# Gated cross-attention and FP4 feed-forward on one core: bias products summed by VectorE, the weights' power applied at the copies, another order of the first tiles

## What is computed

```python
# attention
kp = ctx @ Wk.T;  vp = ctx @ Wv.T + bv;  qp = layernorm(x) @ Wq.T + bq
probs = softmax(qp @ kp.T / sqrt(512))
x = x + tanh(g_xattn) * ((probs @ vp) @ Wo.T + bo)
# feed-forward, 512 -> 1408 -> 512; q4 rounds blocks of 16 to FP4 values
h = silu(q4(layernorm(x)) @ q4(w_gate).T) * (q4(layernorm(x)) @ q4(w_up).T)
x = x + tanh(g_ffn) * (q4(h) @ q4(w_down).T)
```

## Time and profile before

| | |
|---|---|
| median of 3 runs | 832.83 us (832.35 to 833.42) |
| span of the profiled execution | 832.3 us |
| TensorE busy | 822.4 us, 99% |
| VectorE busy | 650.7 us, 78% |
| ScalarE busy | 459.9 us, 55% |
| GpSimd busy | 400.5 us, 48% |
| granted TensorE clock, mean | 1.000 of full speed |
| chain that ended last: TensorE's share | 93% |
| of it `product` (L1918) / `down` (L2037) | 60% / 27% |

### The profile page before, as it was taken

The page is one execution under the profiler, slowest core; times in us unless marked ns, Lnnn a source line. Parts: engine busy times, 40 slices in busy tenths (PEclk is TensorE's granted clock), DMA queues, the critical chain, the costliest instruction groups (busy, mean ns, idle before and its releaser), DMA issues.

```text
span 832.3 us, 11653 instructions
## 1 busy us (share of the span) xinstructions
PE 822.4 (99%) x4102; PEld 417.0 (50%) x4102; DVE 650.7 (78%) x967; ACT 459.9 (55%) x930; POOL 400.5 (48%) x333
## 2 busy tenths in 40 slices
PE   9999999999999999999999999999999999999998
PEld 5555445444554445444544454445544454444445
DVE  5887899898998698877878688778876878776654
ACT  2778675547555666456563755366646565344320
POOL 3498797764334353444333543454444533444421
PEclk9999999999999999999999999999999999999999
DMA  9723703553243434532641255224433443222232
GB/s 318 285 70 103 157 13 97 122 128 92 48 80 106 108 82 89 129 56 54 114 120 40 55 110 136 61 60 99 97 61 61 85 85 73 58 54 55 48 75 73
DMA packets 192817, 78.21 MB, mean 94 GB/s; under 512 B 176387, under 2 KB 178037, under 8 KB 192759
## 3 DMA queue, kind: packets, MB, share of 16 engines
q1 hardware_dynamic: 192759, 77.47, 39.6%
HBM read 22.76 MB, written 8.39 MB: 37 GB/s over the span
## 4 chain that ended last, share of the span: by engine, by line
PE 93%; ACT 3%; DVE 2%; issue 1%; DMA 1%; POOL 1%; POOLq 0%; ACTq 0%; DVEq 0%
PE banks L1918 60%; PE banks L2037 27%; DVE banks L1417 1%; PE banks L2053 1%; PE banks L1912 1%; PE banks L1971 1%; PE banks L1999 1%; PE banks L1998 1%; PE banks L2143 1%; DMA x_T<-x_parts 1%; PE banks L2150 0%; PE banks L2008 0%; PE banks L2160 0%; PE banks L2165 0%; PE banks L2155 0%
## 5 line engine op out<-in xcount | busy, mean ns | idle before, releaser
L1918 PE MATMUL banks<-wgu_hi,x_T 128*128 128x512 f16 (+1 forms) x1536 | 439.3, 361 | 1.6 <-DMA x_T<-x_parts 0.9
L1918 PE MATMUL banks<-wgu_lo,x_T 128*128 128x512 f16 (+1 forms) x768 | 277.5, 361 | 0.0
L1918 PEld LDWEIGHTS banks<-wgu_hi,x_T 128*128 128x128 f16 x1536 | 150.3, 98 | 155.6 <-issue 1.3
L2037 PE MATMUL banks<-wd,arena 128*128 128x512 f16 x1023 | 227.2, 379 | 0.0
L2037 PEld LDWEIGHTS banks<-wd,arena 128*128 128x128 f16 x1023 | 99.7, 98 | 117.4 <-issue 0.6
L648 POOL TENSOR_TENSOR arena<-arena,h_r 128x1024 f32<-128x1024 f32 (+1 forms) x60 | 93.2, 1554 | 115.3 <-DVE h_r L1372 115.3
L648 POOL TENSOR_TENSOR arena<-arena,h_s 128x1024 f32<-128x1024 f32 x64 | 90.7, 1418 | 88.6 <-DVE arena L1419 53.6
L1918 PEld LDWEIGHTS banks<-wgu_lo,x_T 128*128 128x128 f16 x768 | 75.1, 98 | 76.8 <-issue 0.3
L648 POOL TENSOR_TENSOR xwork<-xwork,x_s 128x512 f32<-128x512 f32 x32 | 38.4, 1201 | 152.0 <-DVE xwork L1419 152.0
L1052 ACT ACTIVATE arena<-banks,scal 128x512 f32<-128x512 f32 (+1 forms) x96 | 61.9, 647 | 84.9 <-PE banks L1918 84.8
L1571 DVE SCALAR_TENSOR_TENSOR arena<-arena,scal,banks 128x512 f32<-128x512 f32 (+1 forms) x90 | 62.2, 694 | 56.3 <-PE banks L1918 53.5
(11 more groups left out here) (199 smaller groups left out, 1043.6 us busy)
## 6 DMA issues: line engine op xcount, KB each, us to landing
ring<-in_x_dram SPq DMA_DIRECT2D x8, 1024.0 KB, 5.1
out_dram<-ring SPq DMA_DIRECT2D x31, 256.0 KB, 2.2
arena<-in_L_ffn_w_down_dram SPq DMA_DIRECT2D x4, 704.0 KB, 5.0
arena<-in_L_ffn_w_gate_dram SPq DMA_DIRECT2D x5, 512.0 KB, 9.7
arena<-in_L_ffn_w_up_dram SPq DMA_DIRECT2D x5, 512.0 KB, 9.6
ring<-in_L_xattn_Wk_dram SPq DMA_DIRECT2D x4, 256.0 KB, 6.1
ring<-in_L_xattn_Wq_dram SPq DMA_DIRECT2D x4, 256.0 KB, 6.8
wd<-in_ctx_dram SPq DMA_DIRECT2D x1, 1024.0 KB
```

What stands on the lines that cost most here:

```text
L1918: ended = e.matmul(at, l, r, start=(i == 0), stop=(i == len(terms) - 1))
L2037: ended = e.matmul(by_k(down_ps(t)[:, :], KD), l, r, start=(k == 0 and i == 0), stop=(k == KH - 1 and i == 2))
```

## The change

What it does, part by part:

- **Bias terms.** VectorE sums the four slices of k, each times its bias entries as a per-partition factor (`weighted`: one tensor_scalar, three scalar_tensor_tensor): `bq_sum` over Wk, `key_sum` over the context for both halves at once (616 columns), `bv_sum` over Wo. The sum over partitions is one product with a matrix of ones. The row product of bq, its copy, and the turns go; four products with a one-column moving operand make `bqk_col`. The sums lie in `xn1` and `prob_bytes`, which is why `ln1_apply(0)` and `prob_copy` get a wait. The two bias products of the keys follow each other (`KEY_ORDER`). Wv's load waits for `bq_sum`.
- **Global power.** For pairs 0 to 5 `gu_folds` no longer takes the power, only the constant DOWN, so `gu_times` needs no `pow_ready`. `gu_high` and `gu_low` become activations with the factor `inv_gu`, and the subtracted identity holds minus the power (`neg_p`, one more operation in `gu_power`; `scale_ident` on ScalarE).
- **Squares.** `sum_ps` is renamed `square_ps`; the squares go where they went.
- **Order.** All five lists are ordered anew up to tile 6: among others VectorE has `key_sum`, `scale_bo`, `gu_scales(5)` and `gu_scales(6)` ahead of `gu_top_of`, `gu_round(2)` ahead of `power_of('gu')`, `gu_round(3)` and `gu_round(4)` ahead of `gu_power`; TensorE has `key_product(3)` behind `top_turn('gu')`; ScalarE has `ln1_apply(0)` and `key_copy(5)` behind the first `gu_high`, and `ln1_stats(1)` right ahead of `exps(0)`; SyncE has `x_turn(1)` behind three `move_values`, and the first stores earlier. The loop from tile 7 on is unchanged.

```diff
         ident = sb("ident", [P, P])
-        neg_ident = sb("neg_ident", [P, P], F16)
-        ones = sb("ones", [1, P])
+        neg_ident = sb("neg_ident", [P, P], BF16)
+        ones = sb("ones", [P, P])
...
+        neg_p = sb("neg_p", [P, 1])
...
-        bqk_row = probT[0:1, :]
+        bq_sums = xn1[:, 0, :]
+        key_sums = xn1[:, 1:3, :].rearrange("p i n -> p (i n)")[:, 0:ROWS]
+        bv_sums = prob_bytes[:, :]
...
-        sum_ps = banks[:, 6 * BANK:8 * BANK]
         att_ps = bank[5]
+        square_ps = banks[:, 6 * BANK:8 * BANK]
...
+        KEY_ORDER = [(0, m) for m in range(KD)] + [(0, KD), (1, KD)] + [(1, m) for m in range(KD)]
+        mm = [("key", i) for i in range(KEYS_HALF)] + [("vo", m) for m in range(KD)] + [("bvwo", 0)]
...
             e.dma_start(stage_b, by_rows(Wo)).then_inc(loads["wo"], 16)
-            w.wait_ge(bqk_mm, 1)
+            w.wait_ge(bq_summed, 1)
             e.dma_start(stage_a, by_rows(Wv)).then_inc(loads["wv"], 16)
...
             x_turn(0)
-            x_turn(1)
             move_values(1)
             move_values(2)
-            x_turn(2)
             move_values(3)
-            move_down(0)
+            x_turn(1)
             move_values(4)
             move_values(5)
             move_values(6)
+            move_down(0)
             move_values(7)
+            x_turn(2)
             move_down(1)
             move_down(2)
             move_down(3)
             x_turn(3)
-            h_turn(0)
             w.wait_ge(h_div[1], 2)
             load_x(3)
+            h_turn(0)
             h_turn(1)
             x_turn(4)
...
+            gu_times(0)
             gu_divide(4)
+            gu_times(1)
             gu_divide(5)
             gu_divide(6)
+            gu_times(2)
             ln1(0)
-            gu_times(0)
-            gu_times(1)
-            gu_times(2)
+            gu_divide(7)
             gu_times(3)
-            gu_divide(7)
             gu_divide(8)
             gu_times(4)
-            gu_divide(9)
             gu_times(5)
             gu_times(6)
+            gu_divide(9)
+            gu_divide(10)
             gu_times(7)
             gu_times(8)
-            gu_divide(10)
             gu_low_of(6)
             gu_low_of(7)
+            gu_low_of(8)
             gu_times(9)
-            gu_low_of(8)
             gu_low_of(9)
             x_stats(0)
             gu_times(10)
+            x_stats(1)
+            gu_low_of(10)
...
+                if j0 < MOVED:
+                    e.activation(gu_s[:, cols], gu_s[:, cols], ACT.Copy, scale=DOWN).then_inc(gu_fold, j1 - j0)
+                    return
                 w.wait_ge(pow_ready, NTH["gu"])
                 e.activation(gu_s[:, cols], gu_s[:, cols], ACT.Copy, scale=fold_gu[:, :]).then_inc(gu_fold, j1 - j0)
 
+            def scale_ident():
+                w.wait_ge(consts, IDENT)
+                w.wait_ge(pow_ready, NTH["gu"])
+                e.activation(neg_ident[:, :], ident[:, :], ACT.Copy, scale=neg_p[:, :]).then_inc(negated, 1)
+
             def gu_high(n):
                 w.wait_ge(gu_turned, n + 1)
-                e.copy(wgu_hi[:, gu_at(n), :, :], by_k(bank[gu_bank(n)][:, 0:D], KD)).then_inc(gu_hi, 1)
+                w.wait_ge(pow_ready, NTH["gu"])
+                e.activation(wgu_hi[:, gu_at(n), :, :], by_k(bank[gu_bank(n)][:, 0:D], KD), ACT.Copy, scale=inv_gu).then_inc(gu_hi, 1)
 
             def gu_low(n):
                 w.wait_ge(gu_less, n + 1)
-                e.copy(wgu_lo[:, gu_at(n), :, :], by_k(bank[gu_bank(n)][:, 0:D], KD)).then_inc(gu_lo, 1)
+                e.activation(wgu_lo[:, gu_at(n), :, :], by_k(bank[gu_bank(n)][:, 0:D], KD), ACT.Copy, scale=inv_gu).then_inc(gu_lo, 1)
...
+                if b == 0:
+                    w.wait_ge(bqk_mm, 1)
+                    w.wait_ge(key_mm, KEYS_HALF + 1)
...
             def key_copy(i):
-                j, m = divmod(i, KEYS_HALF)
+                j, m = KEY_ORDER[i]
                 w.wait_ge(key_mm, i + 1)
                 to = keyq[:, m, j * HALF:(j + 1) * HALF] if m < KD else keyb[:, j * HALF:(j + 1) * HALF]
                 e.mul(to, bank[mm_bank["key", i]][:, 0:HALF], SOFT).then_inc(key_sb, 1)
...
-            w.wait_ge(consts, IDENT)
-            e.activation(neg_ident[:, :], ident[:, :], ACT.Copy, scale=-1.0).then_inc(negated, 1)
             gu_squares(0)
             gu_squares(1)
+            gu_folds(0, 2)
...
             w.wait_ge(bqk_mm, 1)
-            e.copy(bqk_row[:, :], bank[mm_bank['bqk_row', 0]][0:1, 0:D]).then_inc(bqk_row_sb, 1)
+            e.copy(bqk_col[:, :], bank[turn_bank['bqk', 0]][:, 0:KD]).then_inc(bqk_sb, 1)
             gu_squares(2)
-            gu_squares(3)
-            w.wait_ge(bqk_turned, 1)
-            e.copy(bqk_col[:, :], bank[turn_bank['bqk', 0]][:, 0:KD]).then_inc(bqk_sb, 1)
             w.wait_ge(loads['gates'], 32)
             e.activation(tanh_a, tanh_a, ACT.Tanh).then_inc(tanh_done, 1)
-            e.activation(tanh_f, tanh_f, ACT.Tanh).then_inc(tanh_done, 1)
-            gu_squares(4)
             key_copy(0)
+            gu_folds(2, 4)
+            gu_folds(4, 5)
+            ln1_stats(0)
             key_copy(1)
-            ln1_stats(0)
+            key_copy(2)
...
             wo_copy(0)
+            gu_squares(3)
             wo_copy(1)
-            key_copy(2)
             key_copy(3)
             wo_copy(2)
+            e.activation(tanh_f, tanh_f, ACT.Tanh).then_inc(tanh_done, 1)
+            key_copy(4)
+            gu_squares(4)
             wo_copy(3)
-            gu_folds(0, EARLY)
+            gu_high(0)
+            scale_ident()
+            key_copy(5)
+            gu_high(1)
+            gu_squares(5)
+            gu_low(0)
             vo_copy(0)
-            key_copy(4)
             ln1_apply(0)
-            gu_squares(5)
-            gu_high(0)
-            gu_high(1)
-            gu_low(0)
+            gu_folds(5, 6)
             xn_copy(0, 0)
+            gu_squares(6)
             gu_low(1)
-            gu_squares(6)
+            gu_folds(MOVED, NPAIR)
             gu_high(2)
+            xn_copy(0, 1)
             gu_high(3)
-            xn_copy(0, 1)
             gu_low(2)
+            gu_squares(7)
             gu_low(3)
             gu_high(4)
             gu_high(5)
             vo_copy(1)
-            vo_copy(2)
-            gu_folds(5, NPAIR)
...
             def gu_power():
                 take_power("gu", p_gu, inv_gu)
                 e.tensor_scalar(fold_gu[:, :], inv_gu, DOWN, None, ALU.mult).then_inc(*step())
+                e.tensor_scalar(neg_p[:, :], p_gu, -1.0, None, ALU.mult).then_inc(*step())
                 e.tensor_scalar(h_fold, inv_gu, H_SHRINK, None, ALU.mult).then_inc(*step())
                 e.tensor_scalar(h_floor, inv_gu, inv_gu, SCALE_FLOOR / H_SHRINK, ALU.mult, ALU.mult).then_inc(pow_ready, 1)
...
-                round_negated(chunk(j)[0], chunk(j)[0], wide_c(j), sum_ps).then_inc(gu_neg, 1)
+                round_negated(chunk(j)[0], chunk(j)[0], wide_c(j), square_ps).then_inc(gu_neg, 1)
...
+            def weighted(to, parts, weights, summed):
+                e.tensor_scalar(to, parts[0], weights[0], None, ALU.mult).then_inc(*step())
+                for i in range(1, KD):
+                    w.wait_ge(dve_step, step.n)
+                    e.scalar_tensor_tensor(to, parts[i], weights[i], to, ALU.mult, ALU.add).then_inc(*((summed, 1) if i == KD - 1 else step()))
+
+            def bq_sum():
+                w.wait_ge(bias_sb, 1)
+                for r in range(KD):
+                    w.wait_ge(loads[f"wkq{r}"], 32)
+                weighted(bq_sums, [stage_a[:, r, :] for r in range(KD)], [bq_col[:, r:r + 1] for r in range(KD)], bq_summed)
+
+            def key_sum():
+                w.wait_ge(bqk_sb, 1)
+                w.wait_ge(ctx_sb, CT)
+                weighted(key_sums, [ctx_T[:, k, :] for k in range(KD)], [bqk_col[:, k:k + 1] for k in range(KD)], key_summed)
+
+            def bv_sum():
+                w.wait_ge(wo_sb, KD)
+                w.wait_ge(bias_sb, 1)
+                weighted(bv_sums, [wo_T[:, r, :] for r in range(KD)], [bv_col[:, r:r + 1] for r in range(KD)], bv_summed)
...
             gu_tops(0)
+            gu_tops(1)
             gu_scales(0)
-            gu_tops(1)
+            gu_scales(1)
             gu_tops(2)
-            gu_scales(1)
             gu_scales(2)
+            gu_round(0)
             gu_tops(3)
-            gu_round(0)
             gu_round(1)
             gu_tops(4)
+            bq_sum()
+            gu_tops(5)
             gu_scales(3)
+            gu_tops(6)
             gu_scales(4)
-            gu_tops(5)
-            gu_tops(6)
             gu_tops(7)
             gu_tops(8)
+            gu_scales(5)
             gu_tops(9)
+            key_sum()
+            scale_bo()
             gu_tops(10)
-            scale_bo()
+            gu_scales(6)
             gu_top_of()
-            gu_scales(5)
-            gu_scales(6)
+            gu_round(2)
```

(73 more changed lines are left out.)

331 lines of the change are left out of this document (164 added, 167 removed).

## The result

| | before | after |
|---|---|---|
| median of the runs, us | 832.83 (832.35 to 833.42) | 869.96 (869.02 to 871.04) |
| ratio | 1 | 1.0442, 95% interval 1.0428 to 1.0457 |
| span of the profiled execution, us | 832.3 | 868.2 |
| TensorE busy, us | 822.4 | 824.8 |
| TensorE idle, us | 9.9 | 43.4 |

The kernel became 4.4% slower; the forecast was 835.8, its range ended at 840. Of the 35.9 us more of span, 10.9 lie ahead of the first product of the hidden layer (the head) and 25.0 behind it (the tiles).

A forecast was written before the change was run, and what follows sets the result against it. TensorE's own work was taken to set the end, with the late global power and ScalarE's queue delaying the head: +5.0 - 1.85 = +3.1 us on 832.8, rounded to 835.8; own range 833.5 to 838.5, eight-in-ten range 827 to 840.

The forecast's parts named there:

- The sign and the order of events in the head: Head: maximum near 40.5, power at 51.9, exps(0) at 85.2, first x_T product at 113.4, 5.0 us later than before.
- VectorE's price: VectorE, head: three sums of 2.6, 3.1 and 2.6 us plus one 0.15 us operation, 8.4 us together.
- outside the case: VectorE sums: all nine two-input steps waiting for GpSimd would put VectorE 17 us further behind; held not to apply.
- My own pair of rows: VectorE: first half of a rounding, 1.28 against 2.74 us, taken to show an operation can double beside GpSimd.
- TensorE as the bound: Whole kernel: TensorE busy 822.4 of 832.3 us, so its own work sets the end.
- The 8.9 us: TensorE, head: work saved on the bq, key bias and bvwo products, 3.43 + 3.1 + 2.57 - 0.2 us.
- rival (1): TensorE's saved work gets through, bounded by gate_up(0) at 104.7: 827.3 us; chance 0.26.
- The scale at the copies: ScalarE, head: 16 weight copies with a per-partition scale cost 0.1 us more each, 1.6 us.
- Rival (3): VectorE becomes the bound up to tile 6, giving back less than some 5 us of idle time: 839.3 us; chance 0.10.
- The order of the tiles: Tiles: finish, h_turn, store and x_turn in the new order save nothing and cost nothing while VectorE's slack holds.
- -1.85 us for waits that go: TensorE, 108.4 to 127.0 us: the wait for x_T at 127.06 and two others vanish, at most -1.85 us.
- my own sign: Profile after: TensorE idle of several us behind 127 would mean VectorE is the bound up to tile 6.

The follow-up runs named there:

- short_sums: The kernel after with its three bias sums cut to their first step, two-input steps left out, every order as in after: 863.8 us, ratio 1.0373.
- power_early: The kernel after with gu_scales(5), gu_scales(6), key_sum and gu_round(2) moved behind power_of on VectorE, gu_power ahead of gu_round(2): 873.9 us, ratio 1.0493.
- bv_sum_alone: The kernel before with bv_sum alone added, placed behind gu_round(6) where VectorE stood idle for 3.07 us: 837.5 us, ratio 1.0046.
- products_cut_alone: The kernel before with the bq, key bias and bvwo products cut to the first of four terms, nothing added: 831.4 us, ratio 0.9989.
- bq_sum_alone: The kernel before with bq_sum alone behind gu_tops(4), with its chain's places in the queues; keys and bvwo as before: 844.2 us, ratio 1.0127.
- new_parts_in_the_old_order: The kernel before, in its own order, with the three sums on VectorE and the scale at the copies: 848.2 us, ratio 1.0182.

## Where the prediction was right and wrong

**The sign and the order of events in the head.** Right: the maximum over the weights late, the power behind it, ScalarE's queue behind that, the first product late. What was to be seen: top_turn('gu') at 40 to 41 with 4 to 5 us of idle time, it was 44.66 with 8.3; the first scaled copy near 52, it was 57.2; exps(0) near 85, it was 90.3; the first x_T product near 113, it was 119.3. Every one is late by the same 4 to 6 us. The steps from the maximum to the first product hold in short_sums: there the maximum ends at 41.6, the first scaled copy stands at 52.2, exps(0) at 85.1 and the first product at 113.3, the forecast's own numbers, though its sums take 1.6 us on VectorE and not the 8.4 of the forecast. But they aren't the only chain: in power_early the maximum ends at 37.75 and the first product comes at 123.1, by way of the folds that wait for VectorE. I had one chain where two run side by side, both through a full VectorE.

**The first term that failed is VectorE's price.** I took 8.4 us, "since GpSimd stands idle at the first and, by my order of events, the third sum". That was right for bq_sum and bv_sum (2.8 each), and key_sum took 4.8 instead of 3.1. Small steps ahead of the maximum were stretched too, two scales by 0.9 us each and the last step of the maximum by 1.0. 0.2 + 1.7 + 1.8 + 1.0 is 4.7; the maximum ended at 44.6, 4.1 later than the 40.5 of the forecast. The rule of the Trainium skill ("SBUF — State Buffer", section "Who interferes with whom"), that a VectorE operation with two SBUF inputs and a GpSimd operation that reads SBUF contend, I had kept outside the case. bv_sum_alone agrees with it: each of the three steps took 2.33 us on average, and 0.78 without GpSimd. My own pair of rows for it, 1.28 against 2.74 us for the first half of a rounding, was read wrongly: GpSimd was multiplying beside the short one too.

```profile
14.79 4.81 POOL L648 TENSOR_TENSOR arena<-arena,valo 128x1024 f32<-128x1024 f32 x2 [3.06 <-DVE valo L1372]
```

These two took 4.81 us instead of 3.83 for two. At 16.52 VectorE kept its time and GpSimd lost; the pair doesn't show GpSimd active against GpSimd idle.

**TensorE as the bound.** Wrong, and it is the lesson of the case. "So the end is set by TensorE's own work" was read from 99% of busy time. products_cut_alone gives 1.5 us for 8.2: in the head TensorE was full and yet not what the end hung on. The 8.9 us stood in my bounds (104.7 at best, and with it rival (1) at 827.3); even with no sum at all that was out of reach in before's order.

**The scale at the copies** was priced at 1.6 us on ScalarE, and the run with it alone measured 1.6 as a whole: right in size, with some luck, since in that run the maximum over the weights also ends 2.4 us later than before.

**Rival (3), VectorE becomes the bound up to tile 6.** Of the rivals this is the nearest to what happened in the head, and I gave it 0.10. Its condition, that VectorE gives back less than some 5 us of its idle time, was met, as the stage from 15 to 70 us shows, of after and of before:

```profile
15.00:70.00 55.00, 38.79 (x152) 22.88 (x150) 52.74 (x65) 31.13 (x68) 31.34 (x18) 0.88 0.42 146
...
15.00:70.00 55.00, 52.36 (x229) 31.06 (x229) 48.98 (x56) 40.25 (x79) 40.31 (x20) 1.00 0.54 191
```

VectorE is busy for 52.74 of 55 us, and its idle time fell by 3.8 us, from 6.0 to 2.3. Its price came through by two thirds in short_sums, 6.1 us for 8.9. In before's order the sums cost 16.3, with 15.0 us more of idle time, and part of that is the order around bqk_col, as bq_sum_alone shows; no step of mine had a term for it. The same 5.35 us wait of ScalarE for bqk_col stands in after.

**The order of the tiles.** The largest miss: "finish, h_turn, store and x_turn in the new order save nothing" and "cost nothing as long as VectorE's slack holds", and -1.85 us for waits that go. Measured: +25.0 behind the first x_T product, 25.5 by itself with before's head. I had checked that nothing waited in the old order, and didn't walk the new one: that x_turn(2) now stands behind move_down(0) and move_values(7), and h_turn(0) behind load_x(3), was in the diff. VectorE's slack did hold as a sum, 24 us idle from 127 to 240 against 12 before, and TensorE waited for VectorE all the same, 4.39 us at 165.42: the sum was the wrong condition. By my own sign TensorE's idle time behind 127, 14.6 us up to 240, would be rival (3); the runs put it down to the order instead.

**A clock term was missing.** With idle time the granted clock falls, to 0.50 in 40 to 50 us and to 0.91 from 140 to 180. Behind the first x_T product the same products take 7.1 us longer, a fifth of the whole loss; the mean clock of 0.98 over 281 us makes 5.6 of it, by my estimate; with before's head and the new order of the tiles it is 9.2 us. My sum had every product at its old length. Filling the gap in the head brought nothing: TensorE had to wait later instead. Whether it would help in the tiles wasn't tried.

Together: 5.9 us too little in the head (10.9 against 5.0), 26.9 in the tiles (25.0 against -1.85), which is the whole of 35.9 against 3.1. (The prediction gives its forecast two ranges, 834.5 to 838 and 833.5 to 838.5; the result is far outside both.)

**Open** stays the share of each moved step in the 25 us: the runs show that they belong to the fit of five queues and that 3.6 hang on one DMA, no more. Also open is what, besides the two-input steps, makes the head 4.8 us late, and how the cost in before's order divides between the sums and the places of their chain. No version that does the whole work was faster than the kernel before; the nearest is the scale at the copies alone, 834.7.

## What to carry to other kernels

An engine that is 99% busy is not thereby the bound: where others deliver just in time, cutting its work makes idle time. Cut the work without adding anything first, it takes one run. In a schedule written out by hand for five in-order queues a new order is never free because nothing waited in the old one: for each moved step ask what now stands at the head of its queue, who holds it, and who is behind. When a new step brings a new order with it, run the order without the step. And price a step on VectorE by who is active on GpSimd in those very microseconds.

## What the runs showed of the hardware

- Three two-input steps of 512 float32 columns on VectorE took 2.32 us with GpSimd idle (after), 3.88 with GpSimd multiplying beside the first of them (new_parts_in_the_old_order) and 6.99 with it beside all three (bv_sum_alone); in after a step of 64 columns took 0.18 without GpSimd and 1.07 beside it, and a step of one column 1.19 beside it, where it took 0.16 without in before.
- After 2.33 and 8.29 us of idle time with one microsecond of work between, the granted clock was 0.50 from 40 to 50 us, the lower of its two levels (1.2 of 2.4 GHz), and a key product took 4.32 instead of 2.34 us. With products that nobody reads in the gap it stayed at 1.00.
- A copy from PSUM with a scale per partition took 0.69 us by itself (0.57 from one to the next) where the plain cast took 0.58 (0.48): a tenth of a microsecond, as estimated.
